# Ternary layers: the low half of a unit's gate and up weights is requested only once its high half has landed

## The reference

```
x = x + 0.5 * ffnA(norm(x));  x = x + attention(norm(x));  x = x + 0.5 * ffnA(norm(x))
x = x + 0.5 * ffnB(norm(x));  x = x + state(norm(x));      x = x + 0.5 * ffnB(norm(x))

ffnA: fwht(silu(x @ W1.T) * (x @ W3.T)) @ W2.T                      # 2048 wide
ffnB: (silu(x @ gate.T * gate_s) * (x @ up.T * up_s)) @ down.T * down_s   # 1408 wide
state: tanh(x @ B.T) @ C.T + D * x
```

## Time and profile before

| | |
|---|---|
| median of 3 runs | 1724.32 us |
| the profiled execution | 1725.91 us |
| its span, first to last instruction | 1724.0 us |
| PE busy | 1703.6 us, 99% |
| DVE, ACT, POOL busy | 67%, 48%, 7% |
| granted TensorE clock | 1.00 throughout |
| chain that ended last | PE 90%, DVE 4%, DMA 1% |
| ffnB: passes 4 and 5; passes 6 and 7 | about 1199 to 1440 us; about 1480 to 1724 us |

### The profile page before, as it was taken

The page is one execution under the profiler, slowest core; times in us unless marked ns, Lnnn a source line. Parts: engine busy times, 40 slices in busy tenths (PEclk is TensorE's granted clock), DMA queues, the critical chain, the costliest instruction groups (busy, mean ns, idle before and its releaser), DMA issues.

```text
span 1724.0 us, 21358 instructions
## 1 busy us (share of the span) xinstructions
PE 1703.6 (99%) x7696; PEld 1391.7 (81%) x7696; DVE 1158.5 (67%) x1802; ACT 823.5 (48%) x1350; POOL 128.8 (7%) x188
## 2 busy tenths in 40 slices
PE   8999999999999999999999999999999999999998
PEld 6788888888888888888888888888787777787786
DVE  8977678677775655754446554457668879867866
ACT  5745534455575543434223333223556455655534
POOL 1000000000012220000000000000000135100001
PEclk9999999999999999999999999999999999999999
DMA  9775555699985000344345344444656652366655
GB/s 331 265 287 214 219 201 195 238 364 367 368 334 202 1 1 1 110 165 163 139 149 197 123 165 154 150 147 154 228 219 234 234 209 104 141 227 228 228 220 221
DMA packets 76235, 340.33 MB, mean 197 GB/s; under 512 B 7904, under 2 KB 18528, under 8 KB 70496
## 3 DMA queue, kind: packets, MB, share of 16 engines
q1 hardware_dynamic: 76128, 338.93, 52.4%
HBM read 259.73 MB, written 79.17 MB: 197 GB/s over the span
## 4 chain that ended last, share of the span: by engine, by line
PE 90%; DVE 4%; POOL 2%; issue 1%; DMA 1%; ACT 1%; SPq 0%; POOLq 0%; ACTq 0%; DVEq 0%
PE psum L520 34%; PE psum L522 29%; PE psum L524 26%; PE psum L761 2%; DVE xc_lo L1883 1%; DMA w<-w_kept 1%; POOL sg L1733 1%; DVE x L1916 1%; POOL x L1734 0%; PE psum L730 0%; POOL rstd L1706 0%; DVE hid L1940 0%; DVE att_lo L1857 0%; PE psum L998 0%; DMA x<-in_w2a 0%
## 5 line engine op out<-in xcount | busy, mean ns | idle before, releaser
L520 PE MATMUL psum<-xc_hi,w 128*128 128x512 f32 x1544 | 610.2, 395 | 4.0 <-DVE psum L1950 2.1
L522 PE MATMUL psum<-xc_lo,w 128*128 128x512 f32 x1544 | 602.4, 390 | 0.0
L524 PE MATMUL psum<-xc_hi,w 128*128 128x512 f32 x928 | 361.3, 389 | 0.0
L520 PEld LDWEIGHTS psum<-xc_hi,w 128*128 128x128 f32 x1544 | 289.9, 188 | 86.2 <-DVE psum L1950 8.3
L520 PE MATMUL psum<-w,hid 128*128 128x512 f32 x864 | 338.2, 391 | 1.6 <-DVE y L1923 0.8
L524 PE MATMUL psum<-w,hid 128*128 128x512 f32 x864 | 336.6, 390 | 0.0
L522 PEld LDWEIGHTS psum<-xc_lo,w 128*128 128x128 f32 x1544 | 290.3, 188 | 56.3
L1916 DVE TENSOR_TENSOR x<-psum,x 128x512 f32<-128x512 f32 x256 | 173.2, 688 | 148.7 <-PE psum L524 148.5
L1940 DVE TENSOR_TENSOR hid<-sg,hid 128x512 fp32r<-128x512 f32 x216 | 149.1, 700 | 99.2 <-ACT hid L1289 94.0
L522 PE MATMUL psum<-w,hid 128*128 128x512 f32 x544 | 211.8, 389 | 0.0
L524 PEld LDWEIGHTS psum<-xc_hi,w 128*128 128x128 f32 x928 | 174.2, 188 | 36.5
(11 more groups left out here) (163 smaller groups left out, 2016.1 us busy)
## 6 DMA issues: line engine op xcount, KB each, us to landing
w<-w_kept SPq DMA_DIRECT2D x186, 896.0 KB, 6.5
w<-w_kept SPq DMA_DIRECT2D x94, 512.0 KB, 7.7
w_kept<-w SPq DMA_DIRECT2D x16, 1792.0 KB, 7.6
w_kept<-prep SPq DMA_DIRECT2D x12, 1792.0 KB, 7.7
w_kept<-w SPq DMA_DIRECT2D x16, 512.0 KB, 6.5
w_kept<-prep SPq DMA_DIRECT2D x12, 512.0 KB, 8.8
att_raw<-in_att_w SPq DMA_DIRECT2D x4, 1024.0 KB, 9.2
x<-in_x SPq DMA_DIRECT2D x4, 1024.0 KB, 12.3
```

Of the source, the lines that this page charges most:

```text
L520: pe.matmul(out, a_hi, b_hi, start=start, stop=False, skip_group_check=onto)
L522: last = pe.matmul(out, a_hi, b_lo, start=False, stop=stop and zero == "a", skip_group_check=onto)
L524: last = pe.matmul(out, a_lo, b_hi, start=False, stop=stop, skip_group_check=onto)
```

## The change

In `w13_load`, for the blocks of the ternary layers (`W13_BASE["B"] <= block < W13_BASE["S"]`), SP waits between the two DMA instructions until the high half has landed. Only then does it issue the low half, and what stands behind it on SP. The amount moved and every other wait stay. The ffnA and state loads are untouched.

```diff
                 sp.dma_start(w13[:, v % 2, 0, :].bitcast(F32),
                              w13_kept[block][:, 0:14 * P]).then_inc(w13_in[v % 2], 16)
+                if W13_BASE["B"] <= block < W13_BASE["S"]:
+                    sp.wait_ge(w13_in[v % 2], nth(n, 2))
                 sp.dma_start(w13[:, v % 2, 1, :].bitcast(F32),
                              w13_kept[block][:, 14 * P:]).then_inc(w13_lo_in[v % 2], 16)
```

## The result

The kernel after takes 1740.34 us (median of 5 runs, 1739.57 to 1745.68) against 1724.31 us before: a ratio of 1.0103, with a 95% interval of 1.0092 to 1.0114. It is slower, by 16 to 18 us. The direction and the place were forecast, the size was not: 11.0 us were forecast, the ratio puts the time at 1742 us, just outside the range, and two of the five runs lie above 1741 us.

The account below looks back on a forecast made before the run. PE, busy 99% of the span, was taken as the bound. Stalls of 2.2 (pass 7), 2.1 (pass 6), 2.6 (pass 5), 3.8 (pass 4) and 0.3 (pass end) sum to 11.0 us: 1724.32 + 11.0 = 1735.3 us, range 1727.5 to 1741.

Parts of the forecast that it names:

- What bounds the kernel: Whole kernel: PE, busy 99% of the span; weight loads charged 13.6 us, but at most 0.4 us could be won.
- The tight place: Slot 3's first down tile in each ternary pass: w2 of block 2, with 1.4 us of slack in pass 4.
- the end of pass 4: w2 of block 10, behind the next pass's unit 0 high half: lands 1312.2, wanted 1311.86, 0.3 us of stall.
- The durations: Landing times on SP's queue: low half 4.7 us; high half's landing to w2's 6.0 us, bounds 5.4 and 6.6.
- pass 4's h2: Landing time of unit 2's high half in pass 4: 7.0 us, giving 3.8 us of stall; with 4.8, 1.5.
- The 2.2 us from the last queued landing to the next high half: SP's queue: from a w2 landing to that of the next high half queued behind it, 2.2 us.
- rival 4: Slower without the clock: pass 5's late unit 3 high half repeats, low halves take 5.3 us; 1742; beyond 16 us, 0.05.
- rival 3: Granted clock falls: one unit at half speed after each of four stalls, 26 us more, 1762; chance 0.05.
- own signs of being wrong: Changed kernel: w well under 6.0 us, PE idle elsewhere, matmuls at a lower granted clock, or an unmoved w2 load.
- A rule weighed: DMA queue: about 2.0 us fixed plus bytes over 436 GB/s; a wait for a landing pays the fixed part anew.
- rival 1: Landings shorten with one load at a time: stalls 3.6 us in sum, 1727.9; chance 0.12.

Follow-up runs that it names:

- The experiment at units 2 and 3: Changed kernel with the wait only in the loads of units 2 and 3 of each ternary pass (8 of 44): 1737.65 us, ratio 1.0076.
- its complement: Changed kernel with the wait in all ternary units but 2 and 3 (36 of 44): 1725.54 us, ratio 1.0003.
- Filled stalls: Changed kernel plus nine matmuls on PE ahead of slot 3's first down tile in each ternary pass: 1737.38 us, ratio 1.0077.
- two-waits kernel: Changed kernel plus a second wait in each ternary load, for the low half's landing, ahead of the w2 load: 1776.58 us, ratio 1.0308.

## Why the prediction was right, and where it was wrong

**What bounds the kernel: right.** The 13.6 us that the chain of waits charges to loads could not be won. Even with the low halves all but gone the time did not move.

**The tight place: right.** w2 of block 2 in slot 3 was named, and 8.6 of the 11.8 us of waits stand there, 2.1 on unit 3's high half just ahead, 1.0 at the end of pass 4. The experiment at units 2 and 3 and its complement show that the other 36 waits cost nothing that the time shows (the 1.0 us at the end of pass 4 came in one of the two profiles), and the one with w2 ahead of the wait shows what they would block.

**The durations: right in sum, and that in part by luck.** The low half, with only a w2 load behind it, landed in a median of 4.8 us (4.7 was taken). From unit 3's high half to w2 of block 2 it took 6.0 us in pass 7 (1637.5 to 1637.88 + 5.6), as forecast. The stalls, without the 0.4 us of before, sum to 11.4 us in one profile and 11.1 in the other (11.0). Singly they were off: pass 4's h2 of 7.0 us did not come back (5.7), so pass 4 lost 2.9 less the old 0.4, 2.5, rather than 3.8; in pass 7 unit 3's high half took 7.5 us and landed 3.5, not 2.2, behind w2 of block 1, so pass 7 lost 3.2 rather than 2.2; the end of pass 4 cost 1.0 rather than 0.3. Those misses cancelled. The 2.2 us from the last queued landing to the next high half came back as 2.2 in passes 4 to 6. The late high half of rival 4 came in pass 7, but its sum did not: 11.4 and 11.1 us of stalls, where it asks for over 16. That its time, 1742, is near the measured one is a coincidence.

**The clock: wrong, and this is the failed step.** The sum left the clock at 1.00 and put its fall at 0.05, as rival 3, with four stalls and 26 us. The ground given, that the clock is 1.00 over the whole stretch, says nothing about stalls that the kernel before does not have; that was seen and still given no weight in the sum, though matmuls at a lower granted clock stand among the prediction's own signs of being wrong. The runs show something between: after stalls of 2.0 to 2.4 us the clock fell in some passes and not in others, once in one profile and three times in the next, each time for 3.4 us. A fall cost 1.7 us, where rival 3 has 6.6. With it the profiles' 14.3 and 17.4 us are accounted for but for 1.2 each. Of that 1.0 and 0.6 us lie behind PE's last matmul, which starts 5.7 us ahead of the span's end before and 6.7 and 6.4 after; the rest is within the 3 us over which runs of the kernel before spread. Filled stalls, at a clock of 0.999 to 1.000, gave 1737.4 us, 12.4 above the kernel before beside it, where 11.0 were forecast. The forecast was thus about the time of the kernel at full clock. The room that its range had up to 1741 was meant for longer landings; those didn't come in sum, and the clock used it up.

**A rule weighed.** A low half that waits for the high half's landing took a whole landing of its own again, 4.8 us in the median, where it used to land 2.2 us behind the high half. The estimate of 4.1 us for 896 KB, worked out from the Trainium skill, DMA: Bandwidth & Descriptors, Anatomy of one DMA (SWDGE path), was too low for this queue. The lighter load on HBM of rival 1 shortened nothing: 4.7 us against 4.8. One account that bears on the clock's chance was left out: the Trainium skill, TensorE: Matmul & The Clock Gate, section HAM oscillation, tells of a matmul kernel whose waits for DMA put the clock down again and again. The two-waits kernel agrees, with up to 14 us lost; the changed kernel, in part.

**What stays open.** What decides whether a stall of 2.0 to 2.4 us brings the clock down: stalls of nearly the same length, in the same place of the same program, did both (pass 7: 2.22 us without a fall, 2.17 with one). Why the kernel with w2 ahead of the wait is slower than before by 0.1%. And why a few engines' shares of a load come 2 us late.

## What to carry to other kernels

A wait put between two transfers delays all that the queue has behind them, so list those, find for each when it is wanted, and compare that with its landing plus one more landing; here one load with 0.4 to 2 us of slack, four times in the program, decided nearly everything, and 36 other waits cost nothing that the time shows. Idle time that a chain of waits charges to a load is not idle time of the engine: read the engine's own waits before hoping for it. And where a change gives TensorE new stalls of 2 us, add time at half clock to the sum, as something that comes in some runs and passes and not in others.

## What the runs showed of the hardware

- The granted clock fell to 0.50 behind four of the eight stalls of 2.0 to 2.4 us in two profiles of the changed kernel, each time for 3.4 us, and with seven of the ten stalls of 1.9 to 4.4 us in the two-waits kernel, at most 14 us lost in sum. After stalls of at most 1.5 us (the wait at unit 3) it stayed up.
- A high half of 896 KB took 4.7 us with 128 KB behind it and 4.8 us with 896 KB behind it (medians of 43): here, what was queued later didn't slow it.
- Behind a queued load, the next 896 KB landed 2.2 us later for unit 3 in passes 4 to 6 of the changed kernel, 3.5 us later in pass 7, and 4.0 us later in pass 4 of the kernel with the small low half (1218.1 to 1222.1), with three of the 16 DMA engines at work from 1220.25 to 1221.5.
